# A last group stored in exchanged order, the weight matrix quantised in two pairs, and the first loads reordered

## What is computed

```python
def _L0_cond_ref(x, conditions, weights):
    w = weights[conditions]
    return jnp.einsum('bct,bcd->bdt', x, w)

def _quant_dequant_mxfp4(x):                       # BLOCK 32, FP4_MAX 6, FP4_EMAX 2
    xb = x.reshape(*shape[:-1], shape[-1] // BLOCK, BLOCK)
    amax = jnp.max(jnp.abs(xb), axis=-1, keepdims=True)
    exp = jnp.floor(jnp.log2(jnp.maximum(amax, tiny))) - FP4_EMAX
    scale = jnp.where(amax > 0, jnp.exp2(exp), jnp.ones_like(amax))
    q = jnp.clip(xb / scale, -FP4_MAX, FP4_MAX)
    lsb = jnp.where(abs(q) < 2.0, 0.5, jnp.where(abs(q) < 4.0, 1.0, 2.0))
    return (jnp.round(q / lsb) * lsb * scale).reshape(shape)

a = _quant_dequant_mxfp4(_L0_cond_ref(x, itok_B_1_198, L0_cond_weights))
w = _quant_dequant_mxfp4(L0_ffn_weight)            # 512 x 512
out = x + jnp.einsum('mk,nk->mn', a, w) + L0_ffn_bias
```

## Time and profile before

| | |
|---|---|
| median of 3 runs | 98.17 us (97.58 to 100.51) |
| the profiled execution | 97.9 us |
| its span, from the first to the last instruction | 96.2 us |
| busy, share of the span: TensorE, VectorE, ScalarE, GpSimd | 88%, 85%, 78%, 34% |
| granted TensorE clock, mean | 0.987 of full speed |
| DMA traffic | 22.17 MB, mean 230 GB/s |
| read from and written to HBM | 10.49 MB, 8.39 MB |

### The profile page before, as it was taken

One profiled execution on the slowest core, in us unless ns is written; L12 is line 12 of the kernel. 1 busy time (PEld: TensorE's weight loads), 2 busy tenths in 40 slices (PEclk: granted clock), 3 DMA queues, 4 the chain that ended last, 5 costly groups with the idle time before them and its releaser, 6 DMA issues.

```text
span 96.2 us, 2263 instructions
## 1 busy us (share of the span) xinstructions
PE 84.4 (88%) x715; PEld 41.2 (43%) x715; DVE 81.9 (85%) x138; ACT 75.3 (78%) x85; POOL 32.9 (34%) x60
## 2 busy tenths in 40 slices
PE   5999594999799998999899899989999989989800
PEld 4966252595482324344233433333352333445300
DVE  1248999999999999999999999999979999885600
ACT  4740498699998869999999999999999849957000
POOL 4273758399647548303000300320040021054000
PEclk9999999999999999999999999999999999999995
DMA  1898789694896789799999991896579399486992
GB/s 34 288 316 295 244 249 301 212 352 125 181 317 218 274 248 269 242 312 265 254 310 298 311 212 49 272 245 116 218 185 224 114 263 222 88 272 175 270 285 92
DMA packets 13901, 22.17 MB, mean 230 GB/s; under 512 B 4034, under 2 KB 4802, under 8 KB 13890
## 3 DMA queue, kind: packets, MB, share of 16 engines
q1 hardware_dynamic: 11456, 17.31, 56.4%
q0 software_dynamic: 2432, 4.73, 23.6%
q10 hardware_dynamic: 2, 0.00, 0.0%
HBM read 10.49 MB, written 8.39 MB: 196 GB/s over the span
## 4 chain that ended last, share of the span: by engine, by line
PE 44%; ACT 11%; DVE 10%; issue 6%; ACTq 0%; DVEq 0%
PE o_ps L357 20%; PE y_ps L357 5%; PE y_ps L306 5%; ACT y_sb L471 5%; ACT o_sb L493 4%; PE o_ps L352 4%; PE o_ps L337 3%; DVE a L654 3%; DVE n_int L625 2%; DVE top L645 2%; ACT z L463 1%; PE o_ps L382 1%; PE y_ps L367 1%; PE y_ps L300 1%; PE y_ps L318 1%
## 5 line engine op out<-in xcount | busy, mean ns | idle before, releaser
L357 PE MATMUL o_ps<-wT,aT 128*128 128x512 bf16 x100 | 23.8, 380 | 0.4 <-ACT aT L508 0.4
L183 POOL DMA_DIRECT2D mix<-in_L_cond_weights_dram x32 | 17.9, 560 | 12.4 <-issue 11.0
L625 DVE TENSOR_TENSOR n_int<-y_sb,inv 128x1024 int16<-128x1024 f32 (+1 forms) x17 | 19.5, 1155 | 0.2
L306 PE MATMUL y_ps<-x_sb,mix 64*64 64x512 f32 x120 | 15.6, 606 | 3.9 <-DMA mix<-in_L_cond_weights_dram 2.4
L272 POOL DMA_DIRECT2D x_sb<-o_sb x6 | 6.1, 1014 | 35.1 <-ACT o_sb L493 35.1
L382 PE MATMUL o_ps<-idle 128*128 128x128 bf16 x214 | 16.6, 235 | 1.2 <-DVE idle L664 1.2
L463 ACT ACTIVATE z<-y_ps 128x1024 bf16<-128x1024 bf16 x16 | 16.2, 1039 | 1.5 <-PE y_ps L306 1.2
L471 ACT COPY y_sb<-y_ps 128x1024 f32<-128x1024 f32 x16 | 16.3, 1035 | 0.0
L382 PEld LDWEIGHTS o_ps<-idle 128*128 128x128 bf16 x214 | 13.6, 105 | 5.1 <-issue 4.7
L480 ACT ACTIVATE zone<-inv 128x1024 int16<-128x1024 int16 (+2 forms) x11 | 11.6, 1074 | 3.8 <-DVE inv L618 3.8
L502 ACT COPY aT<-o_ps 128x1024 bf16<-128x1024 bf16 x14 | 13.7, 1045 | 1.0 <-PE o_ps L337 1.0
(11 more groups left out here) (52 smaller groups left out, 76.0 us busy)
## 6 DMA issues: line engine op xcount, KB each, us to landing
x_sb<-in_x_dram SPq DMA_DIRECT2D x7, 1024.0 KB, 6.4
out_dram<-x_sb SPq DMA_DIRECT2D x15, 256.0 KB, 3.6
x_sb<-o_sb POOLq DMA_DIRECT2D x6, 512.0 KB, 5.2
out_dram<-x_sb SPq DMA_DIRECT2D x6, 512.0 KB, 3.1
w_sb<-in_L_ffn_weight_dram SPq DMA_DIRECT2D x4, 256.0 KB, 3.4
x_sb<-in_x_dram SPq DMA_DIRECT2D x2, 512.0 KB, 6.6
out_dram<-x_sb POOLq DMA_DIRECT2D x4, 256.0 KB, 3.6
mix<-in_L_cond_weights_dram POOLq DMA_DIRECT2D x32, 16.0 KB, 4.5
```

The costliest lines, as they stand in the source:

```text
L183: queue.dma_start(mix[HALVES[i % 2], first + i // 2, :], table[bass.ds(row, 1), :, :].rearrange("o c d -> (o c) d")).then_inc(mix_in[step] ...
L306: last = nc.tensor.matmul(y_ps[HALVES[g], 2 * q + r, :], mix[HALVES[r], (step - 1) * GROUP + n, :], x_tiles(step, n)[HALVES[r], :], start= ...
L357: last = nc.tensor.matmul(o_bank(step, t), aT[:, t, c, :], wT[:, c, :], start=False, stop=(c == KC - 1))
L625: nc.vector.tensor_tensor(columns(n_int, t, n), columns(y_sb[:, step % 2, :, :], t, n), columns(inv, t, n), ALU.mult).then_inc(n_done, 1)
```

## The change

The last group (8) is mixed, added and stored in exchanged order in both pairs: its x is loaded a second time, in exchanged order, into a new buffer `last_x`, at the end of SP's loads. VectorE adds it tile by tile, and each tile is stored in two halves of 64 partitions, one from SP and one from ScalarE's queue. The last group is quantised one tile at a time (zones, rounding, limit, rescale, turning, copying). Group 7 is limited, rescaled and turned in pairs; its first pair goes through `copy_late` as before and is stored by SP; its tiles 2 and 3 are added by VectorE after the last group's rescaling and stored by SP. The upper pair of group 6 is stored by POOL. On TensorE the products of group 6 are moved ahead of group 7's turning, and the PSUM banks are dealt out anew.

W is limited, inverted, rounded and rescaled in two pairs, the first of which starts before the last two pieces of W are through z. `zone_group` becomes `zone_pair`, whose counts are given by the caller. TensorE turns W's first pair ahead of group 2's mixing, and the fillers become 32 and 56 instead of 24 and 60.

SP loads only the first half of group 1's x behind W. The second half is issued by ScalarE after three pieces of W. The table rows of group 2 go out ahead of the x of group 2. `load_mixes` drops the assertions on row numbers.

```diff
@@ loads
+        last_x = sb("last_x", [P, GROUP, T], F32)
...
+        exchanged_x_dram = x.rearrange("(s q g r) c t -> s q g r c t", q=2, g=2, r=2)
...
         def t_pair(step, q):
             if step < LAST - 1:
-                bank = 2 + q
-            else:
-                bank = 2 - q
-            return o_ps[:, bank, :].bitcast(BF16)
+                return o_ps[:, 2 + q, :].bitcast(BF16)
+            return y_ps[:, 3 - q, :].bitcast(BF16)
+        def t_last(t):
+            return o_ps[:, 1 + t % 2, :].bitcast(BF16)[:, 0:K]
...
-                cond_sb[:, 2 * first:2 * (first + len(tiles))], engines=[engine], min_val=0, max_val=S - 1)
+                cond_sb[:, 2 * first:2 * (first + len(tiles))], engines=[engine], min_val=0, max_val=S - 1,
+                skip_runtime_bounds_check_because="cond holds row numbers of the table")
...
+        def store_last(queue, t, g, part, done):
+            queue.dma_start(exchanged_dram[LAST - 1, t // 2, g, t % 2, :, part], last_x[HALVES[g], t, part]
+                            ).then_inc(done, 16)
@@ SP
-            for h in range(2):
-                sp.dma_start(x_tiles(1, 2 * h, 2).rearrange("p (n t) -> p n t", n=2),
-                             x_dram[:, 2 * h:2 * h + 2, :]).then_inc(x_first_in[h], 16)
+            load_first_x(sp, 0)
             sp.wait_ge(cond_in, 16)
             load_mixes(sp, mybir.EngineType.SP, sp_mix_in, 1, SP_TILES)
+            load_mixes(sp, mybir.EngineType.SP, sp_mix_in, 2, SP_TILES)
             load_x(2)
-            load_mixes(sp, mybir.EngineType.SP, sp_mix_in, 2, SP_TILES)
             load_x(3)
...
+            for q in range(2):
+                for g in range(2):
+                    sp.dma_start(last_x[HALVES[g], 2 * q:2 * q + 2, :],
+                                 exchanged_x_dram[LAST - 1, q, g, :, :, :].rearrange("r c t -> c r t")
+                                 ).then_inc(last_x_in, 16)
...
+            for t in range(SUMMED, GROUP):
+                sp.wait_ge(added, t - SUMMED + 1)
+                store(LAST - 1, t)
             for t in range(GROUP - 1):
-                sp.wait_ge(added, t + 1)
-                store(LAST, t)
+                sp.wait_ge(added, t + 3)
+                store_last(sp, t, 0, slice(0, N), stored)
@@ POOL
-            for q in range(2):
-                pool.wait_ge(late_copied, 2 * q + 2)
-                for g in range(2):
-                    pool.dma_start(exchanged_dram[LAST - 2, q, g, :, :, :].rearrange("r c t -> c r t"),
...
+            pool.wait_ge(x_added[(LAST - 2) % 2], 16 * ((LAST - 1) // 2))
+            n0 = (LAST - 3) * GROUP + SUMMED
+            pool.dma_start(out_dram[:, n0:n0 + 2, :], x_tiles(LAST - 2, SUMMED, 2).rearrange("p (n t) -> p n t", n=2)
+                           ).then_inc(late_stored, 16)
@@ TensorE
-                if step == LAST and q == 1:
-                    for n in (2 * q, 2 * q + 1):
-                        for half in HALVES:
-                            last = nc.tensor.matmul(y_ps[half, n, :], mix[half, (step - 1) * GROUP + n, :],
...
-            keep_busy(24)
+            pe.wait_ge(a2_done, 1)
+            turn_pair(0, 0, straight=True)
+            keep_busy(32)
             for q in range(2):
                 mix_pair(2, q)
-            pe.wait_ge(ident_ready, 1)
-            for q in range(2):
-                pe.wait_ge(a2_done, q + 1)
-                turn_pair(0, q, straight=True)
-            keep_busy(60)
+            pe.wait_ge(a2_done, 2)
+            turn_pair(0, 1, straight=True)
+            keep_busy(56)
...
+            for q in range(2):
+                ffn_pair(LAST - 2, q)
             pe.wait_ge(y_copied, tiles_done(LAST, 3))
-            residual_pair(LAST - 1, 1)
-            for t in range(GROUP):
+            pe.wait_ge(a2_done, late_part(0))
+            turn_pair(LAST - 1, 0, straight=True)
+            residual_pair(LAST - 1, 0)
+            for t in range(2):
                 bias_tile(LAST - 1, t, start=False)
-            bias_tile(LAST, 0)
-            for t in range(GROUP):
+            pe.wait_ge(a2_done, late_part(1))
+            turn_pair(LAST - 1, 1)
+            for t in range(2):
+                ffn_tile(LAST - 1, t)
+            pe.wait_ge(aT_ready, tiles_done(LAST - 1, 3))
+            for t in range(2, GROUP):
+                bias_tile(LAST - 1, t)
+            for t in range(2, GROUP):
                 ffn_tile(LAST - 1, t)
-            pe.wait_ge(a2_done, LAST + 2)
-            turn_pair(LAST, 0)
+            pe.wait_ge(pair_copied, 2 * (LAST - 2))
+            bias_tile(LAST, 0)
+            turn_last(0)
+            pe.wait_ge(copied_out, 2 * (LAST - 2))
+            turn_last(1)
+            bias_tile(LAST, 1)
...
+            bias_half(0)
+            pe.wait_ge(aT_ready, tiles_done(LAST, 2))
+            bias_half(1)
             ffn_tile(LAST, 2)
@@ ScalarE
-            for t in range(GROUP):
+            for t in range(3):
                 z_w(t)
-            zone_group(0)
+            load_first_x(act, 1)
+            z_w(3)
+            zone_pair(1, 0)
             for q in range(2):
                 z_pair(1, q)
+            zone_pair(2, 0, 2)
             for q in range(2):
                 y_pair(1, q)
+            for t in range(2):
+                copy_w(t)
             for q in range(2):
                 z_pair(2, q)
-            copy_w(0)
-            copy_w(1)
-            zone_group(1, 0, 2)
+            for t in range(2, GROUP):
+                copy_w(t)
+            zone_pair(after(1), after(0))
             for q in range(2):
                 y_pair(2, q)
...
+            for t in range(GROUP - 1):
+                zone_pair(after(LAST), late_part(1), t, 1)
+            copy_late()
             copy_turned_last(0)
+            zone_pair(after(LAST), late_part(1), GROUP - 1, 1)
+            for t in range(1, GROUP):
+                copy_turned_last(t)
+            for t in range(GROUP - 1):
+                act.wait_ge(added, t + 3)
+                store_last(act, t, 1, slice(0, N), others_stored)
@@ VectorE
+            lowest_zone(1, 0, 2)
+            lift(0, 1, 0, 2)
+            top_zone(1, 0, 2)
+            invert(1, 0, 2)
             tree_1(0, 2, 2, z_count=GROUP)
+            round_w(0)
...
+            invert(2, 2, 2)
             round_w(1)
-            limit(0, 1)
+            limit(0, 2, 2, 2)
             tree_1(1)
-            rescale(0, 1, 2, 2, 2)
+            rescale(0, 2, 2, 2, 2)
...
+            round_y(LAST - 1, 0)
+            round_y(LAST - 1, 2)
+            tree_1(LAST)
+            other_zones(LAST - 1)
+            tree_2(LAST + 3)
+            limit(LAST - 1, after(LAST - 1), 0, 2)
+            tree_3(LAST + 3)
+            rescale(LAST - 1, late_part(0), 2 * LAST, 0, 2)
+            block_max(LAST + 2)
+            limit(LAST - 1, after(LAST - 1), 2, 2)
+            lowest_zone(LAST + 2)
+            rescale(LAST - 1, late_part(1), 2 * LAST, 2, 2)
...
+            round_y(LAST, 0, 1)
+            limit(LAST, after(LAST), 0, 1)
+            for t in range(1, GROUP):
+                round_y(LAST, t, 1)
+                rescale(LAST, late_part(1 + t), 2 * LAST + t, t - 1, 1)
+                limit(LAST, after(LAST) + t, t, 1)
+            rescale(LAST, late_part(1 + GROUP), 2 * LAST + GROUP, GROUP - 1, 1)
+            for t in range(SUMMED, GROUP):
+                dve.wait_ge(o_ready, tiles_done(LAST - 1, t))
+                nc.vector.tensor_tensor(x_tiles(LAST - 1, t), o_bank(LAST - 1, t), x_tiles(LAST - 1, t), ALU.add
+                                        ).then_inc(added, 1)
+            dve.wait_ge(last_x_in, 16 * GROUP)
             for t in range(GROUP - 1):
-                add_residual(LAST, t)
+                dve.wait_ge(o_ready, tiles_done(LAST, t))
+                nc.vector.tensor_tensor(last_x[:, t, :], o_bank(LAST, t), last_x[:, t, :], ALU.add).then_inc(added, 1)
```

239 lines of the change are left out of this document (110 added, 129 removed).

## The result

| | before | after |
|---|---|---|
| median | 98.03 us (97.58 to 100.51, 4 runs) | 96.59 us (96.26 to 97.14, 4 runs) |
| the profiled execution, its span, around it | 97.9, 96.2, 1.7 us | 96.33, 94.3, 2.0 us |
| last addition done | 91.45 us | 89.53 us |
| from there to the end of the span | 4.75 us | 4.8 us |

The ratio of the times is 0.9851, 95% interval 0.9804 to 0.9898: 1.5% less, within the two per cent that the forecast counted as no change. It had said 95.5, 2.7% less, and had given 0.68 to a gain above 2% and 0.27 to what came. The span is 1.9 us shorter, and all of that is there by the last addition; the drain behind it (the time until the last stores have landed) is as long as it was, though two queues now issue the stores. Another 0.3 us is lost outside the span.

A forecast was written before the change was run, and what follows sets the result against it. VectorE bounds the six middle groups, a compute chain and a store drain the tail. Prologue 0, middle 0, hand-over -0.52 and +0.14, last addition 2.1 sooner: span 93.5, plus 1.7 and 0.27, forecast 95.5 us; range 94.2 to 97.3.

The forecast's parts named there:

- First mixing: Prologue, TensorE: mixing starts at 10.6 right behind the warm-up loop, where it had waited for table rows to 11.60.
- The zone behind the z's: Prologue: ScalarE makes the zone of W's second pair after both z's, at 14.6; VectorE waits 0.7 for it.
- Term 0: Prologue: earlier arrival brings nothing at group 1's second tree step, still 16.5; bounds -0.3 and +1.3.
- The middle: Middle groups, 30 to 69 us: VectorE's steps unchanged, the extra megabyte's 3.7 us hidden in 4.3 free DMA time; term 0.
- The cover I named: Middle: no compute instruction waits for the extra x transfers before group 8's additions at 86.
- The terms -0.52, +0.14 and the 2.1 of the tail: Hand-over: no z wait before group 8's tree, -0.52; group 7's limit and rescale halved, +0.14. Tail: last addition gains 2.1.
- The drain: After the last addition: last store issued at 89.4, plus 3.6 gives 93.0; slow drain 93.3 plus 0.7; span taken 93.5.
- the first rival: Tail: the drain binds, all 2.62 MB at the mixed 281 GB/s or slower; span 94.8, time 96.8; chance 0.22.
- The sign I had given for it: Tail, for the first rival: DMA share near 1 from 87 to the end with the last issue after 91.
- the slower rival: Prologue: late x of group 2 lengthens a TensorE hole and the clock falls to half; 100.1; chance 0.04.
- the 0.5 allowed for a slow drain: End of the span: 93.5 taken instead of the 93.0 given by the last store's issue.

The follow-up runs named there:

- the fastest versions: Changed kernel with W's second pair's zone on VectorE and upper pairs of groups 1 to 6 stored by POOL, 0.9671; plus last tile in two stores, 0.9682.

## Why the prediction was right or wrong

The direction, the range and the steps up to the last addition held; the forecast was 1.1 us short, and the step that failed is the drain, and in it the time of the last issue: 89.4 in the forecast, 91.2 in the trace.

- **First mixing** at 10.6: 10.55, right behind the warm-ups. SP's first table row went out at 3.92 (forecast 4.0), the x of group 2 at 9.48 (9.5). The x half from ScalarE's queue went out at 6.15 and took 4.6, to 10.75, against 10.5; group 2's x took 5.6, to 15.1, against 16.1.
- **The zone behind the z's**: wait of 0.7 on VectorE, measured 1.19; the second tree step at 16.5, measured 16.52. Term 0 was right, since the zone came at 14.7 (14.6) and everything behind hangs on it; that VectorE's own work ended at 13.5 and not at 13.9, an estimate in part, only made the wait longer. The run with the zone on VectorE shows the cause as named: take the zone out of ScalarE's queue and the wait is gone. It also shows that the half-microsecond was there to be had, which the forecast had seen and not pursued.
- **The middle**: 0, and VectorE without a pause, 39.00 of 39.00. The DMA share rose from 0.89 to 0.92 only. The reason given, 3.7 us of DMA time against 4.3 free, was not how it went: the rate in this stretch fell (249 to 238 GB/s), because SP's loads ended at 35.5 instead of 42.6 although there are more of them, and more of the bytes moved before 30. With the loads as before the same copy made the accumulations take 7.3 to 7.5. One more megabyte on top (0.99) still stops no engine, but the stores come later. The cover I named, that no compute instruction waits for these bytes, was true; SP's queue and the last accumulation were the ones to look at.
- **Hand-over**: no wait before group 8's tree (73.75), group 8 rounded from 80.27 (80.3). **TensorE**: group 7's products at 79.02 and 81.16, group 8's first at 84.39 (79.0, 81.2, 84.3). **Last addition done** 89.53 (89.3). The terms -0.52, +0.14 and the 2.1 of the tail stand.
- **The drain**: forecast 93.5, measured 94.3. By issue it was to be 89.4 and 3.6 behind it, 93.0, and 0.5 more for a slow drain; it was 91.2 and 3.1. The step reads "nearer the former because three quarters of the bytes are SP's and ScalarE's kind". It took SP's 339 GB/s, measured on stores of 128 partitions, for stores of 64. They run at 218 GB/s from one queue and at 297 to 303 from two, the issues of both queues take up to 0.86 and 1.23 us, and the last goes out at 91.2. By the mixed rate, the first rival, the span would have been 94.8; the measured 94.3 lies between, and the time, 96.59, is nearer to that rival's 96.8 than to my 95.5. The sign I had given for it is there too: a DMA share of 0.93 to 0.95 from 86 on, the last issue after 91. But it is only half that rival. It had all 2.62 MB from 84 on bind, and with 0.52 MB fewer the end stayed where it was; and what makes the rate low is the shape of the stores, not POOL's queue. That the shape also makes the 0.8 us is argued, not shown: whole tiles took 0.7 from the profiled span and nothing that the times can tell.
- The Trainium skill (DMA: Bandwidth & Descriptors, Rules for kernel authors) says that spreading over issuing engines saves only issue time and that one transfer of 128 partitions is to be preferred to two halves. The run with whole tiles agrees on the second (394 against 297 GB/s). The run with one queue leaves the first open: one queue cost 2.0 us of the span, but its issuing (128 KB in 0.60 us) and the engines with lone halves both come to 218 GB/s.
- **Around the span**: 1.7 taken, 2.0 measured, 0.3 of the miss. It was 1.6 to 1.8 in the kernel before and in the three kernels with that zone on VectorE, and 1.9 to 2.1 in all others. Why is open.
- **The clock** stayed at 1.00 to 91 us in the stretches shown and in those from 10 to 20 and 20 to 30, so the slower rival did not come up.

The sum of the miss: 94.3 - 93.5 = 0.8 and 0.3 around the span make 1.1. The 0.27 between the median and the profiled execution was taken over from the kernel before and came out at 0.26, which is luck: nothing ties the one to the other. Luck is also the size of the last step's miss, since 1.8 us of later issue met 0.5 less behind it and the 0.5 allowed for a slow drain.

## What to carry to other kernels

Price the last stores by a row of the same shape and the same queue: number of issues, partitions and bytes, not an average rate. An earlier start of a stage pays only if nothing stands in front of its bound engine's operand in another engine's queue; here 0.43 us of work taken over by the busiest engine itself removed a wait of 1.19, and the fastest versions (0.967 and 0.968 of before) have it. A transfer for which no instruction waits may still make an in-order queue late, so look at when that queue gets to its stores, and load early what is to be hidden.

## What the runs showed of the hardware

- Stores from 64 partitions kept the 16 DMA engines at 0.95 and moved 218 GB/s (from POOL 205 with 0.82); a store from 128 moved 223 with 0.59. In the tail whole tiles made 394 GB/s where halves from two queues made 297, and halves from one queue 217 to 267.
- Issuing a store of 64 to 128 KB took 0.50 to 0.60 us each from one queue, and up to 1.23 from two with the engines at 0.95. Ten from one queue took 6.3 us.
- An accumulating DMA of 512 KB landed in 5.0 us at least and 5.5 in the middle (median) in the changed kernel, in 7.3 and 8.1 where SP's stores went out on top of it and another megabyte was loaded, and in 6.8 and 7.3 where they did so without it.
- With a store in POOL's queue ahead of it, the accumulation landed in 6.5 (median) instead of 5.5.
